# Two chained convolution blocks on one core: the expanding convolution in float32r, and work moved between VectorE and ScalarE

## The reference, cut to what matters

```
# layer 0: a bottleneck with a deformable 3x3 convolution
out    = relu(bn1(conv1x1(x, w1)))               # 1024 -> 256
offset = conv3x3(out, w_off) + b_off             # 256 -> 18: a (dy, dx) for each of 9 taps
val    = sum over 4 corners of gather(out, corner) * bilinear weight     # per tap and pixel
out    = relu(bn2(einsum(val, w2)))              # 9 taps x 256 -> 256
x      = relu(bn3(conv1x1(out, w3)) + x)         # 256 -> 1024, "the expanding convolution"
# layer 1: a masked grouped bottleneck, 4 groups
g = relu(gconv1x1(x * m, w1));  g = relu(gconv3x3(g * m, w2)) * m
y = relu(gconv1x1(g, w3) + x)
```

## Time and profile before

| | |
|---|---|
| median of 3 runs | 2840.26 us |
| the profiled execution | 2831.85 us |
| its span, first to last instruction | 2830.1 us |
| mean granted TensorE clock | 0.995 of 2.4 GHz |
| TensorE busy | 2749.0 us (97%) |
| VectorE busy | 2276.2 us (80%) |
| ScalarE busy | 1225.2 us (43%) |
| GpSimd busy | 1241.1 us (44%) |
| DMA | 864.38 MB, 305 GB/s in the mean |

### The profile page before, as it was taken

The page is one execution under the profiler, slowest core; times in us unless marked ns, Lnnn a source line. Parts: engine busy times, 40 slices in busy tenths (PEclk is TensorE's granted clock), DMA queues, the critical chain, the costliest instruction groups (busy, mean ns, idle before and its releaser), DMA issues.

```text
span 2830.1 us, 39439 instructions
## 1 busy us (share of the span) xinstructions
PE 2749.0 (97%) x12960; PEld 1518.7 (54%) x12960; DVE 2276.2 (80%) x5216; ACT 1225.2 (43%) x2466; POOL 1241.1 (44%) x1159
## 2 busy tenths in 40 slices
PE   8969999999999999999999999999999999999998
PEld 3435555555555555555555555555555555555552
DVE  2148888888888888888888888888889888888871
ACT  1124444444444444444444444444444444444442
POOL 2046544444444444444444444444444555555530
PEclk9989999999999999999999999999999999999999
DMA  8679988889888899888889988889988888888861
GB/s 328 227 278 343 328 304 303 325 325 333 305 312 298 321 331 328 313 314 303 306 326 325 332 305 309 299 326 327 332 306 295 303 316 317 314 317 318 316 230 77
DMA packets 263691, 864.38 MB, mean 305 GB/s; under 512 B 31810, under 2 KB 72898, under 8 KB 255168
## 3 DMA queue, kind: packets, MB, share of 16 engines
q0 software_dynamic: 165888, 604.05, 60.0%
q1 hardware_dynamic: 79168, 190.68, 18.7%
q10 hardware_dynamic: 18432, 67.12, 6.0%
HBM read 747.72 MB, written 114.02 MB: 304 GB/s over the span
## 4 chain that ended last, share of the span: by engine, by line
PE 93%; DVE 4%; issue 1%; DMA 1%; ACT 1%; SPq 0%; POOL 0%; DVEq 0%; POOLq 0%; ACTq 0%
PE psR L529 15%; PE psA L416 15%; PE psD L509 9%; PE psV L490 9%; PE psD L510 9%; PE psD L511 9%; PE psR L563 9%; PE psR L580 5%; PE psR L542 4%; PE psA L457 3%; PE psR L586 3%; DVE val L947 2%; DVE y L930 1%; PE psD L457 1%; PE psA L437 1%
## 5 line engine op out<-in xcount | busy, mean ns | idle before, releaser
L379 POOL DMA_INDIRECT corners<-corner_tables,samples_in x1152 | 1226.2, 1064 | 1489.1 <-DVE val L947 1056.8
L947 DVE SCALAR_TENSOR_TENSOR val<-corners,samples_in,val 128x256 f32<-128x256 f32 x3456 | 1417.3, 478 | 30.0 <-ACT val L697 24.6
L711 ACT ACTIVATE valT_hi<-psV 128x512 fp32r<-128x512 f32 x576 | 311.6, 593 | 912.8 <-PE psD L511 691.9
L957 DVE TENSOR_TENSOR valT_lo<-psV,valT_hi 128x512 fp32r<-128x512 f32 x576 | 370.5, 685 | 239.0 <-ACT valT_hi L711 222.2
L697 ACT ACTIVATE val<-corners,samples_in 128x256 f32<-128x256 f32 x1152 | 490.4, 503 | 32.9 <-DMA corners<-corner_tables,samples_in 29.1
L509 PE MATMUL psD<-valT_hi,w_hi 128*128 128x512 f32 x1152 | 483.4, 420 | 0.4 <-DVE valT_lo L957 0.4
L529 PE MATMUL psR<-deformed,w_sb 128*128 128x512 f32 x1024 | 463.3, 595 | 2.4 <-ACT y L739 1.9
L510 PE MATMUL psD<-valT_hi,w_lo 128*128 128x512 f32 x1152 | 455.6, 396 | 0.0
L511 PE MATMUL psD<-valT_lo,w_hi 128*128 128x512 f32 x1152 | 454.8, 395 | 0.0
L416 PE MATMUL psA<-x_sb,w_sb 128*128 128x512 f32 x768 | 356.7, 603 | 7.4 <-DMA x_sb<-in_x 7.4
L490 PEld LDWEIGHTS psV<-const_sb,val 128*128 128x128 f32 x2304 | 260.3, 142 | 187.2 <-issue 111.8
(11 more groups left out here) (72 smaller groups left out, 1441.5 us busy)
## 6 DMA issues: line engine op xcount, KB each, us to landing
y<-in_x SPq DMA_DIRECT2D x132, 512.0 KB, 7.8
out<-y ACTq DMA_DIRECT2D x128, 512.0 KB
x_sb<-in_x SPq DMA_DIRECT2D x48, 1024.0 KB
corner_tables<-x_sb SPq DMA_DIRECT2D x128, 256.0 KB
corners<-corner_tables,samples_in POOLq DMA_INDIRECT x1152
y<-in_x SPq DMA_DIRECT2D x7, 2048.0 KB, 9.7
corner_tables<-corners SPq DMA_DIRECT2D x8, 1139.0 KB, 4.2
samples_dram<-samples SPq DMA_DIRECT2D x32, 90.0 KB
```

Of the source, the lines that this page charges most:

```text
L379: nc.gpsimd.indirect_dma_start(corners[:, slot, :], None, table, bass.IndirectOffsetOnAxis(ap=index[:, TAPS * t + k:TAPS * t + k + 1], axi ...
L711: nc.scalar.activation(valT_hi[:, m, :], psV[m][:], ACT.Copy).then_inc(valT_ready, 1)
L947: nc.vector.scalar_tensor_tensor(acc, corners[:, n % GS, corner * CMID:(corner + 1) * CMID], samples_in[:, bpar, w:w + 1], acc, ALU.mult, ...
L957: nc.vector.tensor_tensor(valT_lo[:, m, :], psV[m][:], valT_hi[:, m, :].bitcast(F32), ALU.subtract).then_inc(valT_rest, 1)
```

## The change

- conv3's weights are kept as float32r high and low parts (`w3_hi`, `w3_lo`), its input as `def_hi` and `def_lo`; each product of conv3 becomes three float32r matmuls. ScalarE writes the deformed ReLU into borrowed buffers (`gb`, `offs`) and then copies it rounded (`deformed_high`), VectorE subtracts (`deformed_low`, at the end of the step).
- ScalarE scales two corners: the last one in place in `corners`, then the first into `val`. VectorE adds both products of a tap with one instruction on 1024 columns (`add_products`), which waits for all eight scalings, and interpolates two corners instead of three.
- `coordinates` of a block move from the end of step s to tap 2 of step s+1.
- `valT_hi` has two buffers; `valT_copy` waits for the tap before the last, and the wait for the last tap is now valT_low's.
- The expanded mask has one buffer, filled in two halves. The bias and batch-norm inputs lie in `scratch`; the descriptor scratch of dynamic DMAs is 4096 bytes instead of the default 16384.

```
 def conv3(m):
+    chunk = slice(m * P, (m + 1) * P)
     for k in range(MC):
-        mm = pe.matmul(psR[m % 2][:], w3_sb[:, k, m * P:(m + 1) * P], deformed[:, k, :], ...)
+        pe.matmul(psR[m % 2][:], w3_hi[:, k, chunk], def_hi[:, k, :], start=k == 0, stop=False)
+        pe.matmul(psR[m % 2][:], w3_lo[:, k, chunk], def_hi[:, k, :], start=False, stop=False)
+    for k in range(MC):
+        if m == 0:
+            pe.wait_ge(deformed_rest, 2 * c + k + 1)
+        mm = pe.matmul(psR[m % 2][:], w3_hi[:, k, chunk], def_lo[:, k, :], ...)

 def corner0(k):                                   # ScalarE
+    for tile in range(TILES):
+        act.wait_ge(gathered[n % GS], ...)
+        last = corners[:, n % GS, 3 * CMID:]
+        nc.scalar.activation(last, last, ACT.Copy, scale=...).then_inc(first_corner, 1)
     if not fresh:
         act.wait_ge(val_turned, 2 * (TAPS * block + k - 1))
     for tile in range(TILES):
-        act.wait_ge(gathered[n % GS], ...)
         nc.scalar.activation(val[..., tile, :], corners[:, n % GS, 0:CMID], ACT.Copy, scale=...)...

 def valT_copy(k):                                 # ScalarE
-    if k >= 1:
-        act.wait_ge(tap_done, (TAPS - 1) * h + k)
+    if k >= 2:
+        act.wait_ge(tap_done, (TAPS - 1) * h + k - 1)
     ...
 def deformed_relu(o):
+    # waits for offs_turned (o == 1) and for the first half of gconv3 (o == 0)
+    nc.scalar.activation(deformed[o], psD[o][:], ACT.Relu, ...).then_inc(deformed_full, 1)
+def deformed_high(o):
+    act.wait_ge(deformed_full, 2 * h + o + 1)
+    act.wait_ge(conv3_done, KC * h)
+    nc.scalar.activation(def_hi[:, o, :], deformed[o], ACT.Copy).then_inc(deformed_ready, 1)
-last = each(out_relu, 0, 1, 2, 3, 4) + each(deformed_relu, 0, 1) + each(out_relu, 5, 6, 7)
+last = each(out_relu, 0, 1, 2, 3, 4) + each(deformed_relu, 0, 1) + each(deformed_high, 0, 1) + each(
+    out_relu, 5, 6, 7)
 # without A: each(deformed_relu, 0, 1) + each(deformed_high, 0, 1) + each(out_relu, 6, 7)

+def add_products(k):                              # VectorE
+    dve.wait_ge(first_corner, 2 * TILES * (TAPS * block + k + 1))
+    nc.vector.tensor_tensor(acc, acc, corners[:, slot:slot + TILES, 3 * CMID:], ALU.add).then_inc(fma, 1)
 def valT_low(k):
+    if k >= 1:
+        dve.wait_ge(tap_done, (TAPS - 1) * h + k)
     ...
+def deformed_low(o):
+    dve.wait_ge(deformed_ready, 2 * h + o + 1)
+    nc.vector.tensor_tensor(def_lo[:, o, :], deformed[o], def_hi[:, o, :].bitcast(F32), ALU.subtract)...

-c1, c2, c3 = ({k: [corner(k + 1, c)] for k in range(TAPS)} for c in (1, 2, 3))
+c1 = {k: [lambda k=k: add_products(k + 1)] for k in range(TAPS)}
+c2, c3 = ({k: [corner(k + 1, c)] for k in range(TAPS)} for c in (1, 2))
-beside[2] += c1[2] + c2[2] + c3[2]
+beside[2] += c1[2] + c2[2] + c3[2] + [coordinates]
-beside[7] += c1[7] + c2[7] + each(gb_mask, 0, 1) + c3[7]
+beside[7] += c1[7] + c2[7] + each(gb_mask, 0, 1) + each(mask_expand, 1) + c3[7]
 beside[8] += each(out_add, 0, 1) + [positions] + c1[8] + each(
     valT_low, 8) + each(out_add, 2, 3) + c2[8] + each(
-    out_add, 4, 5) + c3[8] + each(out_add, 6, 7) + [coordinates]
+    out_add, 4, 5) + c3[8] + each(out_add, 6, 7) + each(deformed_low, 0, 1)
```

More of the change, by code:

```diff
@@ L768, in step @@
                     }
-                    last = each(deformed_relu, 0, 1) + each(out_relu, 6, 7)
+                    last = each(deformed_relu, 0, 1) + each(deformed_high, 0, 1) + each(out_relu, 6, 7)
                 for k in range(TAPS):
@@ L931, in out_add @@
                                             ).then_inc(out_sum, 1)
+                def add_products(k):
+                    if ("B" if k < TAPS else "next B") not in on:
+                        return
+                    block, bpar = (h, par) if k < TAPS else (h + 1, odd)
+                    k %= TAPS
+                    slot = TILES * (TAPS * bpar + k) % GS
+                    acc = val[:, (bpar + k) % 2]
+                    dve.wait_ge(first_corner, 2 * TILES * (TAPS * block + k + 1))
+                    nc.vector.tensor_tensor(acc, acc, corners[:, slot:slot + TILES, 3 * CMID:], ALU.add
+                                            ).then_inc(fma, 1)
                 def interpolate(k, corner):
@@ L942, in interpolate @@
                         acc = val[:, (bpar + k) % 2, tile, :]
[L943 to L946 removed]
+                        dve.wait_ge(fma, N_FMA * block + FMA_TAP * k + 1 + (tile + 1 if corner == 2 else 0))
                         nc.vector.scalar_tensor_tensor(acc, corners[:, n % GS, corner * CMID:(corner + 1) * CMID],
@@ L949, in interpolate @@
                                                        ).then_inc(fma, 1)
+                def deformed_low(o):
+                    if "B" not in on:
+                        return
+                    dve.wait_ge(deformed_ready, 2 * h + o + 1)
+                    if low > LAG_B:
+                        dve.wait_ge(conv3_done, KC * h)
+                    nc.vector.tensor_tensor(def_lo[:, o, :], deformed[o], def_hi[:, o, :].bitcast(F32), ALU.subtract
+                                            ).then_inc(deformed_rest, 1)
                 def valT_low(k):
@@ L987, in step @@
                     beside[5] += c1[5] + c2[5] + c3[5]
-                    beside[6] += c1[6] + c2[6] + each(gb_mask, 0, 1) + c3[6]
+                    beside[6] += c1[6] + c2[6] + each(gb_mask, 0, 1) + each(mask_expand, 1) + c3[6]
                     beside[7] += c1[7] + c2[7] + c3[7] + [positions]
-                    beside[8] += c1[8] + c2[8] + each(valT_low, 8) + c3[8] + [coordinates]
+                    beside[8] += c1[8] + c2[8] + each(valT_low, 8) + c3[8] + each(deformed_low, 0, 1)
                 if low == LAG_B:
-                    for c in range(1, 4):
+                    add_products(0)
+                    for c in (1, 2):
                         interpolate(0, c)
```

166 lines of the change are left out of this document (96 added, 70 removed).

## The result

The changed kernel takes 2930.84 us (median of 4 runs, 2929.91 to 2935.01), the kernel before 2840.22 (4 runs, 2838.16 to 2841.08): ratio 1.0324, 95% interval 1.0308 to 1.0341. It is 3.2% slower; the forecast was 2927. The profiled execution takes 2931.02 us, its span is 2928.8.

The account below looks back on a forecast made before the run. TensorE, busy 97% of the span, was taken as the bound. 2831.85 + 41 (full steps) + 46 (closing steps) = 2919 us profiled, median 8.4 above: 2927 us; range 2820 to 2975.

Parts of the forecast that it names:

- The ring: VectorE's addition waits for eight ScalarE scalings, y_adds stand behind it, y_relu and next scalings behind those; 10.87 us once walked.
- the sign: Whole kernel: slower 0.83, same 0.04, faster 0.13.
- The full step: Steps in which all stages run: stalls +4.4 us against -2.57, net +1.8; 22 of them and step 9, +41 us.
- turn 3: TensorE's turn before tap 3 in a full step: waits 1.14 + 0.17 us for valT_low, which stands behind the coordinates.
- The closing step: Last eight steps, deformed block but no first convolution: stalls 10.5 us against 2.1 before, less 2.57: +5.8 each, +46 us.
- The coordinates: VectorE, tap 2: 2.60 us between the last interpolation of tap 3's values and valT_low(2), on which turn 3 waits.
- The second turned buffer: valT_copy need not wait for the tap before: between 0 and 11 us, frees ScalarE earlier in taps 5 to 8.
- Float32r conv3: TensorE: conv3 in three float32r products, -2.57 us a step, worth 82 us if nothing else moved.
- The ends: Start and tail of the execution: the first corners +2 us, the last conv3 -2 us.
- The ring does not bind: Rival, chance 0.13: TensorE stays the bound; all stalls gone, median 2758 us; only full steps' gone, median 2827.
- Gathers late: Rival, chance 0.15: ScalarE reads corners earlier, slots freed no earlier; one to two us a step, median 2957 to 2987.
- the rule of the Trainium skill: Each VectorE addition could wait for a gather's 0.94 us issue, up to 9 us a step; given no chance.

Follow-up runs that it names:

- the best order: Changed kernel with y_adds ahead of additions, coordinates after valT_low(2), and closing steps' out_relu(4, 5) behind tap 1's scalings: 2790.97 us, ratio 0.9819.
- the two reorderings: Changed kernel with y_adds ahead of additions and coordinates after valT_low(2): 2797.18 us; that kernel with closing steps' out_relu(4, 5) behind tap 1's scalings: 2790.97 us.

## Why the prediction was right, step by step

**The ring and the sign.** The waits came where they were walked, and the experiments show that the ring is the cause: one corner instead of two (-118 us), or the same work in another order (-134 us), each turns the loss into a gain.

**The full step.** +1.85 us measured (83.74 to 85.59), +1.8 forecast. By place, forecast and measured (a stalled instruction's start, less the start of the one ahead and its pitch; 0.13 more for each stalled turn): turn 1 0.82 and 0.69, turn 3 1.31 and 1.30, conv3(6) 0.47 and 0.47, conv3(7) 0.86 and 0.73, gconv1 0.66 and 0.40, its second half 0.47 and 0.45. Turn 3, for one: 1818.39 - (1816.75 + 2 x 0.233) = 1.17, and 0.13. Together 4.59 and 4.04: the waits were over-forecast by 0.55. By them the step would have grown by 4.04 - 0.12 - 2.57 = 1.35; this step is 85.42 us long from one conv3(0) to the next, the shortest of its kind, so 1.68 more than before. The 0.33 between the two are small terms that the sum lacked. The largest is that conv3(6) and conv3(7), which start after a stall, take 0.34 for their first matmul (1822.67 to 1823.01) and not 0.233, 0.22 together; for the first matmul after transposes, 0.32, nothing is to be added, since the transposes ahead of it take 0.08 less. The rest was not traced. So the ring and its places were right, and that the full step came within 0.05 is luck in part: two errors of about half a microsecond stood against each other.

**The closing step.** +5.67 measured (72.85 to 78.52), +5.8 forecast; additions at 0.10, 10.05, 19.88 and 28.00 after conv3(0), forecast 0.17, 10.27, 20.17 and 28.34.

**The coordinates.** Booked inside turn 3's wait, 1.31 a full step, 30 us in 23. The run without the move is 45 us faster and its full step 1.65 shorter: undersized. In that run's full step the gaps at turn 3, conv3(6), conv3(7) and the first half of gconv1 are gone and conv3(3) has a new one of 0.71, so what stands behind turn 3 was late with it too; and 5 of the 45 us are in the first closing step, which the prediction did not price.

**The second turned buffer: booked at "between 0 and 11 us" by the rows of the kernel before, worth 64.** The sum did not suffer, since the walk had the copies at their new place. What was wrong is the reason given: the earlier trace rows prices a wait in the old order, where ScalarE had nothing behind it that anyone needed soon. Eight scalings now stand there.

**Float32r conv3.** -2.57 a step came as forecast on TensorE and was nearly all lost to the ring (7 us left of 82, and these within the noise). The prediction's sum subtracts it from the waits, which holds only where the lateness is read against TensorE's own progress, as the walk did.

**The ends.** The profiled execution rose by 99.2 us, 87 was forecast; the 8.4 us by which the median stood above it before was not there after (2930.84 and 2931.02), so that 2927 is nearer to the median than its own terms deserve. The 11.7 us that the span's forecast lacks: start 2.7, full steps 2.4, the last eight 5.3 (4.2 of it in the first, which is 90.33 long where it was 80.39, and 2.6 in the second; the other six gave 1.5 back), tail 1.3. TensorE's clock fell in the first steps and in these two, told below; whether that is the reason stays open. That the forecast of the median is 4 us off and not 12 is luck.

**The rivals.** "The ring does not bind" is excluded by the gaps above; the price that it had for the case of no stalls, 2758, was not reached even by the best order, 2791. "Gathers late" did not happen: ScalarE waits 28.3 us for gathers in the changed kernel, 29.1 before. No holding up of VectorE by GpSimd, one side of the rule of the Trainium skill (SBUF — State Buffer, "Who interferes with whom"), shows either: the 288 additions take 1219 ns in the mean and none more than 1266, as the 1.22 of the earlier trace rows. The other side, GpSimd held up by the additions, does show, and is told in the last section.

## What to carry to other kernels

Moving work from a busy engine to an idle one moves its completion too: before counting the saved microseconds, ask what the moved work's consumer waits for now (here eight scalings instead of one) and what stands behind that consumer in its queue. Where waits follow from order, walk each in-order queue with durations from the trace; it gave both periods of the changed kernel within 0.3 us, though with errors of half a microsecond that cancelled, and pointed to the two reorderings that turned 3.2% slower into 1.8% faster. Price a buffer or a faster operation in the kernel that has it, by a run that undoes it there: the same conv3 was worth 7 us, not clear of the noise, inside the ring and about 60 outside, and a wait that was priced at 11 us at most from the rows of the kernel before cost 64 in the changed one.

## What the runs showed of the hardware that was not expected

**The clock.** TensorE's granted clock fell to half, which is 1.2 GHz, more often than in the kernel before. Windows of the changed kernel (stretch, its length, busy us by engine with counts; clock, DMA share, GB/s), first the start of the deformed blocks, then the first closing step:

```profile
308.00:312.00 4.00, 2.05 (x9) 1.32 (x7) 3.96 (x10) 3.79 (x9) 0.57 (x1) 1.00 0.94 374
312.00:316.00 4.00, 3.42 (x13) 3.12 (x14) 3.96 (x8) 3.00 (x8) 3.08 (x4) 0.57 0.61 178
...
2211.00:2217.00 6.00, 2.29 (x9) 0.60 (x8) 4.94 (x11) 3.67 (x7) 2.04 (x2) 0.99 0.83 279
2217.00:2223.00 6.00, 5.38 (x13) 4.14 (x14) 5.71 (x12) 1.00 (x2) 4.86 (x4) 0.50 0.96 302
2223.00:2234.00 11.00, 8.65 (x45) 7.04 (x44) 6.51 (x13) 7.18 (x15) 3.66 (x4) 0.97 1.02 411
2234.00:2237.00 3.00, 3.00 (x8) 1.94 (x7) 2.55 (x5) 1.61 (x4) 2.15 (x2) 0.50 0.43 142
```

TensorE is busy 2.05 of 4 us and 2.29 of 6, and then runs at 0.57 and 0.50. The kernel before at the same two places was busy 2.46 of 4 us and stayed at 1.00, and 5.23 of 8 and fell to 0.66 once:

```profile
308.00:312.00 4.00, 2.46 (x17) 1.91 (x16) 4.00 (x10) 2.67 (x6) 2.60 (x3) 1.00 0.98 314
312.00:316.00 4.00, 3.70 (x15) 2.32 (x13) 4.00 (x12) 1.12 (x3) 3.39 (x3) 1.00 0.92 332
...
2160.00:2168.00 8.00, 5.23 (x20) 2.77 (x20) 7.10 (x15) 6.12 (x13) 1.21 (x1) 1.00 0.70 252
2168.00:2173.00 5.00, 4.45 (x7) 1.93 (x8) 4.76 (x18) 0.93 (x2) 2.81 (x3) 0.66 0.91 261
```

At the lower level conv3's matmuls are 0.43 apart instead of 0.23:

```profile
2217.62 0.77 PE L544 MATMUL psR<-def_hi,w_hi 128*128 128x512 f32 x1 [2.96 <-ACT y L779]
2218.19 0.63 PE L545 MATMUL psR<-def_hi,w_lo 128*128 128x512 f32 x1
2218.62 0.63 PE L544 MATMUL psR<-def_hi,w_hi 128*128 128x512 f32 x1
```

By windows of 2 us, length times what the clock lacks of 1.00, summed from 260 us to the start of the tail (2860 us in the changed kernel), TensorE lacks 11.9 us so in the changed kernel, 1.7 in the kernel before, 18.8 in the run with additions by tile, 15.4 in the one with the coordinates back, and 5.1 and 8.5 in the two fastest of the two-corner runs.

This is what TensorE lacks and not what the execution loses. A closing step of the changed kernel at 1.00, and one of the run with the coordinates back, in which the clock fell once (it shows 0.59 over the 4 us from 2436):

```profile
2463.50:2542.00 78.50, 70.62 (x349) 43.58 (x348) 61.93 (x119) 50.36 (x111) 38.96 (x37) 1.00 0.84 299
```

```profile
2436.00:2514.50 78.50, 71.71 (x349) 44.80 (x349) 61.94 (x120) 50.74 (x111) 41.54 (x36) 0.98 0.83 296
```

TensorE is busy for 1.1 us more, and both steps are 78.52 long: a wait behind the fall took it up. So a fall of the clock behind a wait need not cost the execution anything. The first closing step, 90.33 us with three falls in the changed kernel and 85.40 with one in that run, is where it may have cost something. That the clock makes up the 11.7 us above is not shown.

**Gathers beside additions.** GpSimd's issue of a gather, 0.94 us for most, was longer beside VectorE's subtractions and additions of two operands in SBUF. At the start of a full step it takes 3.23 us while VectorE does both subtractions of the split and an addition:

```profile
1790.15 0.68 DVE L1013 TENSOR_TENSOR def_lo<-gb,def_hi 128x512 fp32r<-128x512 f32 x1
1790.15 3.23 POOL L392 DMA_INDIRECT corners<-corner_tables,samples_in  x1 [0.30 <-issue]
...
1791.35 1.22 DVE L988 TENSOR_TENSOR val<-val,corners 128x1024 f32<-128x1024 f32 x1
```

In the one-corner run, whose VectorE does the two subtractions at this place and no addition, it takes 2.09:

```profile
1822.74 2.09 POOL L392 DMA_INDIRECT corners<-corner_tables,samples_in  x1 [0.30 <-issue]
```

Between 400 and 2100 us 41 of 728 issues of the changed kernel took more than 1.35 us, 1.75 to 3.24, and every one of them met an addition; in the kernel before, which has neither these subtractions nor the additions, it was 2 of 747. VectorE's own times did not change (1205 to 1266 ns for an addition). GpSimd is not the bound here and ScalarE's wait for gathers did not grow, so that nothing was lost. The one-corner run has other issues of 1.7 to 2.9 beside interpolations and masks, which were not traced.
